# Self attention of a decoder layer: from the third batch the q, k and v projections become three rounded F32 products, with the splitting on GpSimd

## What is computed

```
qkv = x @ w_qkv.T                                  # 512 x 256 by 256 x 768, per batch
q, k, v = split into 16 heads of 16
scores = einsum('bhqd,bhkd->bhqk', q, k) * scale + bias
attn = softmax(scores); out = einsum('bhqk,bhkd->bhqd', attn, v)
out = out @ w_proj.T + b_proj
x = layernorm(x + out)
```

## Time and profile before

| what | value |
|---|---|
| median of 3 runs | 1072.94 us (1064.57 to 1075.15) |
| profiled execution, its own time | 1077.01 us |
| span of its trace | 1074.8 us |
| mean granted TensorE clock | 0.936 of full speed |
| one self body with its projections | 48.8 us, from one to the next |
| the self bodies, the cross bodies, the experts | to about 421, 717 and 1075 us of the span |

### The profile page before, as it was taken

The page is one execution under the profiler, slowest core; times in us unless marked ns, Lnnn a source line. Parts: engine busy times, 40 slices in busy tenths (PEclk is TensorE's granted clock), DMA queues, the critical chain, the costliest instruction groups (busy, mean ns, idle before and its releaser), DMA issues. The chain is left out here.

```text
span 1074.8 us, 17314 instructions
## 1 busy us (share of the span) xinstructions
PE 957.4 (89%) x5205; PEld 512.4 (48%) x5205; DVE 673.9 (63%) x1760; ACT 772.3 (72%) x1452; POOL 320.7 (30%) x326
## 2 busy tenths in 40 slices
PE   5599999999999999999999999982399988988982
PEld 2233433334343433333333333332398887988871
DVE  5276777777777777354355565645378676866763
ACT  1387778777877778898799889850287866768761
POOL 4021112131211111001122212212326656666564
PEclk9699999999999999999899999975599988999996
DMA  8998696978769485696496559400523333433341
GB/s 208 199 232 232 137 241 141 318 156 225 210 144 274 99 207 112 153 251 121 93 164 138 106 111 177 99 20 23 182 102 112 106 112 124 155 119 116 119 160 64
DMA packets 73543, 162.89 MB, mean 152 GB/s; under 512 B 16441, under 2 KB 40056, under 8 KB 63416
## 3 DMA queue, kind: packets, MB, share of 16 engines
q1 hardware_dynamic: 68088, 152.23, 56.9%
q0 software_dynamic: 5056, 9.20, 3.0%
q10 hardware_dynamic: 320, 0.52, 0.1%
HBM read 116.40 MB, written 49.54 MB: 154 GB/s over the span
## 5 line engine op out<-in xcount | busy, mean ns | idle before, releaser
L698 ACT ACTIVATE probs<-sc 128x512 f32<-128x512 f32 x1024 | 528.5, 608 | 118.7 <-DVE sc L780 83.7
L484 PE MATMUL sc<-qst,kst 57*128 57x512 f32 (+1 forms) x1024 | 269.2, 474 | 18.9 <-DMA qst<-s_qk 12.9
L780 DVE TENSOR_TENSOR sc<-sc,strip 128x308 f32<-128x308 f32 (+1 forms) x512 | 192.8, 430 | 106.2 <-PE sc L484 105.9
L484 PEld LDWEIGHTS sc<-qst,kst 57*128 57x128 f32 (+1 forms) x1024 | 118.7, 187 | 206.9 <-ACT probs L698 162.5
L496 PE MATMUL ot<-probs,vals 128*32 128x512 f32 x1600 | 214.1, 607 | 0.0
L1714 POOL DMA_INDIRECT f_rows<-s_x,f_get_ids x45 | 104.4, 2320 | 35.2 <-issue 23.3
L1572 ACT ACTIVATE f_h<-f_h_ps,f_par 128x384 f32<-128x384 f32 x104 | 64.0, 615 | 26.4 <-PE f_h_ps L1491 26.3
L1652 DVE TENSOR_TENSOR f_h_lo<-f_h,f_h_hi 128x384 fp32r<-128x384 f32 x104 | 57.0, 548 | 27.4 <-ACT f_h_hi L1573 26.7
L517 PE MATMUL ms<-xT,w_qkv 128*128 128x512 f32 x128 | 67.0, 653 | 4.6 <-DMA w_qkv<-in_w_qkvT 2.4
L496 PE MATMUL ms<-probs,vals 128*32 128x512 f32 x448 | 64.7, 654 | 0.0
L1573 ACT ACTIVATE f_h_hi<-f_h_ps,f_par 128x384 fp32r<-128x384 f32 x104 | 64.3, 618 | 0.0
(11 more groups left out here) (157 smaller groups left out, 1561.4 us busy)
## 6 DMA issues: line engine op xcount, KB each, us to landing
s_qk<-w_hi SPq DMA_DIRECT2D x32, 512.0 KB, 7.3
strip<-in_w_all SPq DMA_DIRECT2D x16, 1024.0 KB, 12.6
f_raw<-in_w_all SPq DMA_DIRECT2D x14, 1024.0 KB
kst<-s_qk SPq DMA_DIRECT2D x32, 256.0 KB, 6.0
qst<-s_qk SPq DMA_DIRECT2D x32, 256.0 KB, 7.3
s_x_parts<-split SPq DMA_DIRECT2D x16, 512.0 KB, 8.7
kst<-s_ctx_parts SPq DMA_DIRECT2D x32, 256.0 KB, 6.3
qst<-s_x_parts SPq DMA_DIRECT2D x32, 256.0 KB, 7.7
```

The source lines that it names most:

```text
L484: nc.tensor.matmul(sc[j][:], kst[at:at + rows, i, P * c:P * c + P], qst[at:at + rows, i, :], start=True, stop=True).then_inc(scored, 1)
L698: nc.scalar.activation(probs[:, k % KEPT, j, :], sc[j][:], ACT.Exp, scale=scale).then_inc(exped, 1)
L780: nc.vector.tensor_tensor(sc[j][:, lo:hi], sc[j][:, lo:hi], band_backwards(rank_of(4 * g + j), at, hi - lo), ALU.add).then_inc(biased, 1)
```

## The change

For batches 2 to 7 the projections read rounded parts: `w_qkv_hi`, `w_qkv_lo`, `x_hi`, `x_lo`, all F32R. Each F32 product becomes three F32R products, hi by hi, hi by lo and lo by hi, so a block that took two products now takes six. Batches 0 and 1 keep the F32 products. POOL makes the parts: the weights once, in body 0 (`split_weights`, 128 x 1536 twice), and x in body b for batch b + 2 (`split_x`, 128 x 1024 twice), ahead of `copy_v` of groups 0 to 2. `project_qk(b, 0)` waits for the low part of x. SP's wait ahead of the load of `xT` is, from body 1 on, for the split of the batch before instead of for `v_mm`; its place in the queue is the same. `w_qkv_hi` lies in the free half of the buffer `split`.

```diff
+        w_qkv_hi = four[:, 0:2].rearrange("p i s n -> p (i s n)")[:, 0:DC * 3 * C].rearrange("p (d n) -> p d n", d=DC)
...
+        x_hi, x_lo = sb("x_hi", [P, DC, N], F32R), sb("x_lo", [P, DC, N], F32R)
+        w_qkv_lo = sb("w_qkv_lo", [P, DC, 3 * C], F32R)
...
                 if b < B - 2:
-                    sp.wait_ge(v_mm, 2 * (b + 2))
+                    if b == 0:
+                        sp.wait_ge(v_mm, 4)
+                    else:
+                        sp.wait_ge(x_lo_ready, b)
                     sp.dma_start(xT[:], io["xT"][b + 2].rearrange("(c p) n -> p c n", p=P)).then_inc(ld_xT, 16)
...
+            def terms_of(b):
+                if b < 2:
+                    return [(w_qkv, xT, d) for d in range(DC)]
+                return [(w, x, d) for d in range(DC) for w, x in ((w_qkv_hi, x_hi), (w_qkv_hi, x_lo), (w_qkv_lo, x_hi))]
+
             def project_qk(b, i):
                 if i == 0:
                     wait(pe, ld_xT, 16 * b)
+                    wait(pe, x_lo_ready, b - 1)
+                    if b == 2:
+                        pe.wait_ge(w_halved, 1)
                     wait(pe, v_nat, 2 * b)
...
-                for d in range(DC):
-                    last = nc.tensor.matmul(ms[i % 2][:], w_qkv[:, d, col:col + P], xT[:, d, :],
-                                            start=(d == 0), stop=(d == DC - 1))
+                terms = terms_of(b)
+                for n, (w, x, d) in enumerate(terms):
+                    last = nc.tensor.matmul(ms[i % 2][:], w[:, d, col:col + P], x[:, d, :],
+                                            start=(n == 0), stop=(n == len(terms) - 1))
                 last.then_inc(qk_mm, 1)
...
+            def split_weights():
+                pool.wait_ge(ld_w, 16)
+                pool.wait_ge(ld_wv, 16)
+                nc.gpsimd.tensor_copy(w_qkv_hi, w_qkv[:]).then_inc(w_hi_done, 1)
+                pool.wait_ge(w_hi_done, 1)
+                nc.gpsimd.tensor_tensor(w_qkv_lo[:], w_qkv[:], w_qkv_hi.bitcast(F32), ALU.subtract).then_inc(w_halved, 1)
+
+            def split_x(b):
+                pool.wait_ge(ld_xT, 16 * b)
+                wait(pool, v_mm, 2 * b)
+                nc.gpsimd.tensor_copy(x_hi[:], xT[:]).then_inc(x_hi_ready, 1)
+                pool.wait_ge(x_hi_ready, b - 1)
+                nc.gpsimd.tensor_tensor(x_lo[:], xT[:], x_hi[:].bitcast(F32), ALU.subtract).then_inc(x_lo_ready, 1)
...
                 x_and_bias(b)
+                if b == 0:
+                    split_weights()
+                if b < B - 2:
+                    split_x(b + 2)
                 for g in range(G - 1):
                     copy_v(b + 1, g)
```

More of the change, by code:

```diff
@@ L231, in attention @@
         judged = sem("judged")
+        w_halved, x_hi_ready, x_lo_ready, w_hi_done = sem("w_halved"), sem("x_hi_ready"), sem("x_lo_ready"), sem("w_hi_done")
         halted, fresh = [ctx.enter_context(nc.semaphore(f"halted{i}")) for i in range(4)], ctx.enter_context(nc.semaphore("fresh"))
@@ L526, in project_v @@
                     wait(pe, out_read, 2 * (b - 1))
[L527 to L530, removed]
+                tok = P * (2 * i + t)
+                terms = terms_of(b)
+                for n, (w, x, d) in enumerate(terms):
+                    last = nc.tensor.matmul(ms[1 - i][:, C * t:C * t + C], x[:, d, tok:tok + P], w[:, d, 2 * C:3 * C],
+                                            start=(n == 0), stop=(n == len(terms) - 1))
                 if t == 1:
```

## The result

The changed kernel took 1066.71 us in the median of 20 runs (1061.98 to 1072.53), the kernel before 1072.99 us on the same chip (20 runs), a ratio of 0.9948 [0.993, 0.9965]: about 6 us less, 0.5%. The profiled execution took 1071.02 us, of which the span has 1069.2.

The account below looks back on a forecast made before the run. PE alone was taken to bind steps 0 to 3, the DVE and ACT round as much as PE in steps 9 and 10. 1077.0 - 8.4 - 1.8 + 4.9 = 1071.7 profiled; 1067.6 us from the median; range 1060 to 1077.

Parts of the forecast that it names:

- q and k: Projection blocks in steps 0 to 3: six F32R products, 1.37 us for 1.72, 0.35 less per block, 8.4 us over 24.
- The experts' products: Model for the F32R products: 384 columns, 128 x 128 weights, 0.1734 us apart, giving 0.229 us for 512 columns.
- exposed loads: Rival: weight loads add 0.12 us to each of six products per block; 1100.6 us in all; chance 0.04.
- v: project_v blocks: 0.15 us less each, 3.6 us at most over 24 blocks; half taken, 1.8, range 0 to 3.6.
- The waits: PE waits for the split of x at step 0 of bodies 1 to 6, 2.2 us in body 1, together 4.9.
- issue + landing + split - wanted: Sum giving each wait at step 0: x load's issue, time to landing, 3.51 us of POOL's split, less PE's wanting.
- no `weigh` waits for the copies: Copies of the values behind POOL's split end about 1.2 us after it, 4.6 us ahead of their first user; no cost.
- Nothing covers that: Step 0: later PE work stands behind the waiting product, so the waits of 4.9 us are lost in full.
- the rival: The wait is hidden: all waits at step 0 go and v gains in full, 12.0 us, 1060.9; chance 0.12.
- The clock: Rival: PE's clock falls at the new stall in each of six bodies, 21.6 us on top, 1089 us; chance 0.13.
- one fall at two blocks: Price of a clock fall in a body: two projection blocks 1.8 us slower each; from three bodies against the change.
- POOL's work at nothing: Weights' split, about 5.3 us once in body 0, and POOL's other work, lying earlier or later, cost nothing.

Follow-up runs that it names:

- e7: Changed kernel with project_v back in F32 products, split and wait kept, SP's x load also waiting for project_v: 1070.23 us, 0.9974 of the kernel before.
- e8: Changed kernel with project_qk back in F32 products, split and wait kept, SP's x load also waiting for project_v: 1077.13 us, 1.0059 of the kernel before.
- e9: The changed kernel run again unedited, side by side with e10: 1070.14 us, 0.9969 of the kernel before.
- e5: Kernel of e4, but POOL's split of x also waits for DVE's norm_x of the batch before: 1065.76 us, 0.9929 of the kernel before.
- e10: The kernel of e5 run again, side by side with e9: 1067.24 us, 0.9931 of the kernel before.
- e6: Kernel of e1, but POOL's split of x also waits for DVE's norm_x of the batch before: 1069.28 us, 0.9971 of the kernel before.
- e4: Kernel of e1, plus batch 2's x loaded in body 0 already, into the unused buffer of x1: 1082.82 us, 1.0075 of the kernel before.
- e1: Changed kernel with SP issuing the load of x ahead of the store of x1 (batches 3 to 7): 1086.1 us, 1.011 of the kernel before.
- e2: Changed kernel with all products back in F32, split and wait kept, SP's x load also waiting for project_v: 1080.05 us, 1.0062 of the kernel before.
- e3: Changed kernel with POOL's subtraction in the split of x done twice (2.4 us more): 1095.31 us, 1.0166 of the kernel before.

## Why the prediction was right

**q and k.** Predicted: products 0.229 us apart, 0.35 us per block, 1.40 per body. Measured: 0.2325 apart, 0.32 per block, 1.27 per body (e7), so 7.6 us instead of 8.4. The experts' products were the right model, and the weight loads of 128 columns, one per product, do not show: exposed loads would have made the distance 0.35. That rival is out, and with it, for this form, the rule of the Trainium skill ("TensorE: Matmul & The Clock Gate", Part 3) that the prediction weighed: taken alone it says that the blocks would not have shrunk (the same part of the page also names a load into the background weight buffer as one that overlaps, and no run here tells whether these loads are of that kind).

**v.** Predicted 0.30 per body, half of the full 0.60, between bounds of 0 and 0.60. Measured 0.42 (e8), 2.5 us in six bodies instead of 1.8. Blocks shrank by the full 0.15 and part came back as longer scores: that two of the four steps are bound elsewhere was right, but not which: in body 4 the scores behind the first and the last block took 0.14 and 0.15 us longer (1.04 and 0.94 us to the next `weigh` instead of 0.90 and 0.79), those behind the two between at most 0.03, and the scores of the step after were 0.18 shorter (2.10 instead of 2.28).

**The waits.** Predicted 2.2, 0.5, 1.1, 0.4, 0.4, 0.3, together 4.9. Measured 1.88, 0.66, 1.38, 0.59, 0.55, 0.69 (5.75), and 5.37 in e9. The sum "issue + landing + split - wanted" holds place by place, the late one in body 3 too. The steps behind it stood as well: no `weigh` waits for the copies, and SP's wait for the split of the batch before moved nothing (the issue at 225.05 stands behind the same store as before).

**The step that fails**: "Nothing covers that". In the shortened step ACT covers the first 0.33 us in bodies 2 to 6 (e5). This doesn't change the sum of the changed kernel, since products and wait were each priced on the same path (48.8 - 1.74 + wait = 47.04 + wait). It changes the rival: with all waits gone the time is not 1060.9 but 1065 to 1066 by the ratios (e5, e10). Of the 4 to 5 us between, 5 x 0.33 = 1.65 of the waits were never there to win, 1.9 are the smaller gains of the products (7.6 + 2.5 instead of 12.0), and the rest, about 1 us, is less than the intervals leave open.

**The clock.** The prediction gave it 0.13 and wrote "0.3 to 0.5 us are shorter than waits for ACT of up to 1.6 us"; that held in bodies 2 to 6. In body 1 it fell. Body 1 took 50.24 us, against 45.94 in e6, where x came in time. Compared step by step on PE, 1.9 of these 4.3 us are the wait, and 1.5 are the half rate: the block takes 2.63 us from 88.06 to 90.69 instead of 1.60, and the scores behind it 1.11 instead of 0.66. The remaining 0.85 us come from the clash told below, ahead of the stall. So the sum lacks 1.5 us of half rate and 0.85 us of the clash in this execution, and 2.6 and 0.36 in e9.

The prediction had priced one fall at two blocks, 3.6 us. It took that price from the earlier trace rows and read the slow block there as a fall of the clock after a stop of 2.13 us. That reading was wrong: the clock was at its lower level from 26.83 us on, within a wait of PE of 12.88 us for q, and that stop only ended at 39.09. The stretch ahead of the stop in the kernel before, columns as in the earlier trace rows:

```profile
26.83:36.90 10.07, 1.17 (x4) 0.53 (x4) 0.26 (x1) 0.00 (x0) 0.00 (x0) 0.50 0.96 203
```

By that price two such bodies (7.2 us), not three, would already have outweighed the gain of 5.3.

In the two profiles six bodies gain only 291.34 - 289.32 = 2.0 us where 5.3 was forecast, 1.8 in e9's, and 6.3 with e6's body 1 in the place of this one. Both profiled executions of the changed kernel have the stall; how many of the others have it is not known. By the ratios the whole program gains 5.6 us in the first comparison and 3.3 in e9. Two executions of the same kernel also differ by 2.8 us in body 0, ahead of the six (47.48 us here, 44.65 in e9). That the median lies within 1 us of the forecast is thus in part luck and no proof of each term; the periods are. About 3 of the 6 us by which the profiled executions differ lie behind the last `project_v`; in the cross attention the kernel before had a fall of the clock in the stretch from 526 us where the changed kernel has none, as the prediction warned.

**Not seen.** The prediction put POOL's work at nothing: the weights' split "is done once in body 0", and "its other work in the body lies earlier or later". The weights' split did cost something. DVE's `normed`, a product of two tiles in SBUF, met it in the changed kernel (POOL's subtraction; then DVE's bias adds and `normed`):

```profile
68.12 3.47 POOL L1236 TENSOR_TENSOR w_qkv_lo<-w_qkv,split 128x1536 fp32r<-128x1536 f32 x1
```

```profile
69.16 0.84 DVE L799 TENSOR_TENSOR sc<-sc,strip 128x308 f32<-128x308 f32 x2
69.91 1.96 DVE L815 TENSOR_TENSOR normed<-turned,rden 128x256 f32<-128x256 f32 x1
```

`normed` took 1.96 us instead of 0.41 and ended 0.3 us behind the subtraction; the two bias adds beside it, on blocks in PSUM, kept their 0.84. The scores from 73.35 on took 0.84 us longer than at the same step of e6, where the weights' split had ended at 65.36, ahead of `normed`; with 1.47 us for `normed` it was 0.36 longer in e9, and with 2.12 it was 1.0 longer in e10. The kernel before shows the same clash, with the split of the context, so it could have been seen ahead:

```profile
384.18 2.36 POOL L1189 TENSOR_TENSOR ctxT<-ctxT,ctx_hi 128x1024 fp32r<-128x1024 f32 x1
```

```profile
385.01 1.81 DVE L796 TENSOR_TENSOR normed<-turned,rden 128x256 f32<-128x256 f32 x1
```

That the split of x was harmless where it stood was luck of the order: 6 us earlier it would have run into `norm_x`, at a price of 15 us (e4 against e5, e1 against e6, by the ratios). The prediction looked for collisions on POOL's own queue and not for what POOL does to DVE.

## What to carry to other kernels

A load that feeds a new step must be timed against the step's wanting, place by place: issue, landing, work, and wanting, each from its row, gave six waits within 0.4 us. Before such a load is moved up, look at what DVE does at the moment when POOL will then work; here a POOL instruction of 2.4 us on SBUF held a DVE instruction of 0.4 us on SBUF for all its length, and in a loop that goes round through DVE, ACT and PE this cost more than the wait that was removed. Take a wait's price as its length less what the next engine in the ring needs anyway.

## What was not expected of the hardware

A `TENSOR_SCALAR` of DVE on 128 x 256 F32 in SBUF takes 0.41 us, and 2.52 with a `TENSOR_TENSOR` of POOL (2.36 us) that starts at the same time; the first cast of the split, 1.04 us, became 1.21 in e1 where it met `norm_x`, which took 1.45 instead of 0.73.

Two loads of 512 KB on one queue, issued 0.67 us apart, took 11.1 and 14.2 us; the second took 4.3 in e6 and 4.9 in e2, where the first was issued 8.35 and 6.2 us ahead of it.

PE's clock stayed at full speed in bodies 2 to 6 after idle times of up to 1.45 us at step 0 (e2), and went to its lower level in body 1 after 1.49 (e8, where the next block took 3.37 us instead of 1.98), 1.55 (e1), 1.88 and 2.07; in e3 it went there in every body, after 2.82 us and more. The idle times on the two sides come within 0.04 us of each other, and what else differs between body 1 and the others was not tried.
